# Cross attention with LoRA on one core: VectorE evicts each projected group one slot later in its order

## The reference

```python
def _lora_linear(x, W, A, B):
    return x @ W + SCALING * (x @ A @ B)
q = _lora_linear(hidden_states, Wq, Aq, Bq).reshape(bsz, q_len, NH, HD)
k = _lora_linear(traces, Wk, Ak, Bk).reshape(bsz, t_len, NKV, HD)
v = _lora_linear(traces, Wv, Av, Bv).reshape(bsz, t_len, NKV, HD)
...
scores = jnp.einsum('bhqd,bhtd->bhqt', q, k) / jnp.sqrt(jnp.asarray(HD, q.dtype))
attn = jax.nn.softmax(scores, axis=-1)
context = jnp.einsum('bhqt,bhtd->bhqd', attn, v)
out = _lora_linear(context, Wo, Ao, Bo)
return hidden_states + out
```

## Time and profile before

| | us |
|---|---|
| time, median of 3 runs (680.14 to 681.97) | 681.96 |
| time of the profiled execution | 681.03 |
| its span, first to last instruction | 678.9 |
| start-up and end outside the span | 2.1 |
| first T(4) to the last batch's T(4), seven batches | 414.3 |
| PE busy | 661.4 (97%) |
| DVE busy | 519.4 (77%) |
| ACT busy | 466.9 (69%) |

### The profile page before, as it was taken

How to read it: one execution, slowest core, us unless ns; L and a number is a source line. 1 busy time by engine, 2 the same in 40 slices (tenths; PEclk the granted TensorE clock), 3 DMA queues, 4 the chain that set the end, 5 groups by cost and what they waited for, 6 DMA issues and landing times.

```text
span 678.9 us, 14783 instructions
## 1 busy us (share of the span) xinstructions
PE 661.4 (97%) x4220; PEld 526.2 (78%) x4220; DVE 519.4 (77%) x1173; ACT 466.9 (69%) x1462; POOL 368.4 (54%) x316
## 2 busy tenths in 40 slices
PE   8999999999999999999999999999889999999998
PEld 6787777877887787787788788777666788888886
DVE  4868889788788778878877887878887898855542
ACT  5557888888888888888888888887678443222220
POOL 3548734852772484376258437635867005876632
PEclk9999999999999999999999999999999999999999
DMA  9957665774666477466657756667576234655331
GB/s 277 342 167 206 196 194 148 211 206 137 182 208 185 143 220 209 152 172 199 183 159 197 209 160 180 203 186 215 181 227 208 104 123 166 207 185 186 124 121 65
DMA packets 103797, 124.67 MB, mean 184 GB/s; under 512 B 9280, under 2 KB 85312, under 8 KB 103760
## 3 DMA queue, kind: packets, MB, share of 16 engines
q1 hardware_dynamic: 103760, 124.23, 60.5%
HBM read 86.18 MB, written 38.01 MB: 183 GB/s over the span
## 4 chain that ended last, share of the span: by engine, by line
PE 80%; DVE 9%; ACT 4%; DMA 3%; issue 2%; SPq 1%; POOL 0%; DVEq 0%; ACTq 0%; POOLq 0%
PE banks L1481 19%; PE banks L1674 17%; PE banks L1479 10%; PE banks L1499 8%; PE banks L1529 7%; PE banks L1516 7%; PE banks L1540 6%; DVE neg_max L1137 2%; ACT banks L906 2%; PE banks L1460 2%; PE banks L1446 2%; DVE turned_sb L1158 1%; PE banks L1447 1%; DMA q_parts<-q_stage 1%; DVE x_both L1178 1%
## 5 line engine op out<-in xcount | busy, mean ns | idle before, releaser
L906 ACT ACTIVATE banks<-banks,neg_max 128x256 f32<-128x256 f32 x512 | 230.2, 453 | 40.2 <-DVE neg_max L1137 32.4
L790 POOL TENSOR_TENSOR q_stack<-turned_sb,head_mask 8x512 fp32r<-8x512 f32 x128 | 138.5, 1082 | 185.3 <-DVE turned_sb L1158 179.1
L1137 DVE TENSOR_REDUCE neg_max<-banks 128x2 f32<-128x512 f32 x256 | 174.4, 684 | 30.1 <-PE banks L1499 28.7
L917 ACT ACTIVATE probs_t<-banks 128x512 f32<-128x512 f32 x256 | 155.1, 606 | 41.2 <-PE banks L1516 40.5
L1481 PE MATMUL banks<-x_both,w_hi 128*128 128x512 f32 x448 | 164.2, 398 | 1.1 <-DVE q_stage L1131 1.1
L1479 PE MATMUL banks<-x_both,w_lo 128*128 128x256 f32 x448 | 118.5, 280 | 0.0
L1499 PE MATMUL banks<-k_stack,q_stack 96*128 96x256 f32 x512 | 109.7, 296 | 2.1 <-DMA q_stack<-q_parts 2.0
L1499 PEld LDWEIGHTS banks<-k_stack,q_stack 96*128 96x128 f32 x512 | 80.7, 189 | 35.4 <-issue 17.6
L906 ACT ACTIVATION_READ_ACCUMULATOR banks<-banks,neg_max 128x1 f32 x512 | 107.3, 209 | 0.0
L1516 PE MATMUL banks<-q_stack,k_stack 104*128 104x512 f32 x256 | 101.6, 397 | 0.0
L1481 PEld LDWEIGHTS banks<-x_both,w_hi 128*128 128x128 f32 x448 | 83.1, 189 | 14.8 <-DVE q_stage L1131 3.4
(11 more groups left out here) (156 smaller groups left out, 1149.3 us busy)
## 6 DMA issues: line engine op xcount, KB each, us to landing
q_stack<-q_parts SPq DMA_DIRECT2D x192, 128.0 KB, 3.0
q_parts<-q_stage SPq DMA_DIRECT2D x64, 256.0 KB, 3.7
raw<-ct SPq DMA_DIRECT2D x32, 256.0 KB, 4.2
raw<-xt SPq DMA_DIRECT2D x32, 256.0 KB, 3.9
scales<-r_rows SPq DMA_DIRECT2D x64, 128.0 KB
context<-ctx_stage SPq DMA_DIRECT2D x64, 128.0 KB, 3.9
stage<-xn SPq DMA_DIRECT2D x16, 512.0 KB, 4.9
w_hi<-context SPq DMA_DIRECT2D x14, 512.0 KB, 7.0
```

The costliest lines, as they stand in the source:

```text
L790: nc.gpsimd.tensor_tensor(q_stack[rows, u % RING, heads], turned_sb[rows, u % 2].unsqueeze(1).broadcast_to([M_ROWS, 2, S]), head_mask[rows ...
L906: last = nc.scalar.activation(score_bank(s)[:, S * h:S * (h + 1)], score_bank(s)[:, S * h:S * (h + 1)], ACT.Exp, bias=neg_max[:, u % 2, i: ...
L917: nc.scalar.activation(probs_t[:, u % 2, t, 2 * hp:2 * hp + 2, :].rearrange("p a b -> p (a b)"), st_bank[j % 2], ACT.Exp, scale=-1.0).then ...
L1137: nc.vector.tensor_reduce(out=neg_max[:, u % 2, 2 * c:2 * c + 2], in_=score_bank(s).rearrange("p (h t) -> p h t", h=2), axis=AXIS, op=ALU. ...
```

## The change

In the first batch and in the loop, DVE evicts a group in slot e + 2 in place of e + 1, directly behind that slot's row maximum and ahead of everything else in the slot. The v1 group moves from the end of slot 3 to behind the row maximum of slot 4, in every batch, the last one too. The other groups of the last batch stay. No instruction is added or taken away, and PE, ACT, POOL and SP keep their order.

```diff
@@ proj_lows
-                    if end_slot(i, last) + 1 == s:
+                    if end_slot(i, last) + (1 if last else 2) == s:
@@ slot (vector)
                     row_max(b, s + AHEAD - 1)
-                if last:
-                    proj_lows(b, s, last)
+                proj_lows(b, s, last)
+                if s == FIRST + 1:
+                    (narrow_low if first else proj_low)("v", 1, 1, b * PER + (PRO - 1), None, b)
                 here = u >= 0 and not (last and u >= NG)
...
                 if s < FIRST:
                     return
-                if s == FIRST:
-                    (narrow_low if first else proj_low)("v", 1, 1, b * PER + (PRO - 1), None, b)
                 if first and s in LORA_O_SLOTS:
                     build_stack_o(LORA_O_SLOTS.index(s))
-                if not last:
-                    proj_lows(b, s, last)
-                    if s in LOW_SLOTS:
-                        j = LOW_SLOTS.index(s)
-                        input_low(x_hl, j, x_hi_done, x_ready, b * 4 + (j + 5))
+                if not last and s in LOW_SLOTS:
+                    j = LOW_SLOTS.index(s)
+                    input_low(x_hl, j, x_hi_done, x_ready, b * 4 + (j + 5))
```

## The result

The changed kernel takes 687.42 us (median of 4 runs, 686.77 to 688.73), the kernel before 681.69 us beside it (4 runs, 680.14 to 681.97). The ratio is 1.0096, 95% interval 1.0079 to 1.0112: slower by about 5.7 us, where 681.8 was forecast and 683.9 was the end of the range. The profiled execution of the changed kernel took 688.73 us, of which 2.2 lie outside its span, against 681.03 for the one of before: 7.7 us apart.

A forecast was written before the change was run, and what follows sets the result against it. PE, busy for 97% of the span at full clock, was taken as the bound. On the profiled 681.03 us, 3.5 - 1.5 - 1.0 - 0.3 + 0.1 = +0.8 us gave 681.8 us, range 679.6 to 683.9.

The forecast's parts named there:

- In the changed order slot 15 opens with its row maximum: Slots 15 to 19: DVE's gapless chain runs 0.18 us later, so k0's eviction makes slot 19's matmul 0.38 us late.
- The bound from above, 0.5: Slot 19: the most its matmul was expected to be late in a pass, in us, against 0.38 forecast.
- Slot 33 ... is the template of the changed slot.: Slot 33's v0 eviction already follows a row maximum; its timings, second start 0.61 us after the first, were applied to changed slots.
- step-0 price: Slots 11, 27 and 35: groups starting at step 0 begin 0.07 us late in each pass.
- The upper bound of 0.19: Slots 11, 27 and 35: the lateness in us if the matmul is delayed by as much as its load.
- Rival 3: Slower: the four step-0 starts pay the whole load's delay and slot 28's waits stay; 685.7 us at the far end; chance 0.20.
- Slot 24, -1.5 us: Loop, slot 24: the wait behind q0's eviction goes, since row maxima no longer queue behind it; 0.25 us in six passes.
- Slot 28, -1.0 us: Loop, slot 28: scores' waits for q0's stack shrink because slot 20's turning comes some 0.6 us earlier; bound: nothing goes.
- First batch, -0.3: First batch: slot 11 pays +0.6, slot 24's 0.48 goes, slots 27 and 32 keep half of 0.9; bounds -1.0 and +0.7.
- Last batch, +0.1: Last batch: the first fold waits 0.8 us longer for v1, less 0.66 us of the next fold's wait.
- Rival 5, Clock (0.02): Several small PE gaps a pass lower the granted clock to 1.2 GHz for one four-slot unit; at most 688 us; chance 0.02.
- What would show it: Right: alike passes of 58.9 to 59.2 us; wrong: differing passes, or slot 19's wait near zero or over 0.8 us.

The follow-up runs named there:

- turn_reversed: The changed kernel with DVE's four transposes of a unit in opposite order, the last one reading partitions 0 to 31; 685.01 us, ratio 1.0041.
- its control: The kernel before with only the order of its four turning instructions reversed; 681.32 us, ratio 0.9997.
- pool_after_low: The changed kernel, but GpSimd waits before its third input_high (slot 16) until DVE has done the first input_low; 687.42 us, ratio 1.0093.
- v1_early: The changed kernel, but v1 is evicted in slot 3 as before, in all batches; 690.13 us, ratio 1.0119.
- slack_late: The kernel before with only q4, q6, k1, q0, q2 and q3 evicted one slot late; 679.24 us, ratio 0.9984.
- v1_late_last: The kernel before, but in the last batch alone v1 is evicted in slot 4 behind the row maximum; 681.99 us, ratio 1.0015.

## Why the prediction was wrong, by its steps

- **"In the changed order slot 15 opens with its row maximum ..., does the same work, and is 0.18 later."** This is the step that failed. The chain from slot 15 to 19 was taken as a sum of DVE's own durations, moved as a block. It is not: moved by 0.30 us (T(15) + 2.12 for 1.82), its input_low asks for SBUF together with GpSimd's third high part (T(15) + 2.09) and lasts 1.56 us for 0.68 in four of the six passes. Slot 19 cost 5.8 us in the loop instead of 2.3. Of the 3.5 us missed the collision is 3.0 (four times 0.76), the hold of the next point the rest. Shown by the two kinds of pass, by the four passes of q7 late alone, and by turn_reversed, where input_low comes 0.18 late as predicted, the collision is gone and slot 19 costs 0.34. GpSimd's 3.60 us for three high parts stood in the trace of before; I never laid it beside DVE's timeline. The bound from above, 0.5, came from DVE and PE alone, so the range could not hold the truth.
- **"Slot 33 ... is the template of the changed slot."** Wrong for q: the eviction behind a row maximum starts 0.72 us after it, 0.61 for v. The step-0 price is 0.18 to 0.19 at slots 11 and 27 and 0.05 at slot 35, so 1.1 us each instead of 0.4. The same 0.11 us also carried input_low past GpSimd's start. The upper bound of 0.19 held. Shown by turn_reversed, with its control.
- **Rival 3, the nearest to what came**, set the same 0.19, but for another reason, the matmul delayed with its load. Its point of decision, a pass grown by 0.35 us, was passed (0.6 to 1.5 over the shortest pass). Its far end, 685.7, lay outside the range I gave; its "683.8 with half of it" is halfway from 681.8 to 685.7, not the sum with half of the 6.4, which is 682.5.
- **Slot 24, -1.5 us**: right in size, -1.7. That it follows from q0's own move is wrong: q0 late alone leaves 0.16 to 0.37, k0 late alone 0.04 to 0.11.
- **Slot 28, -1.0 us**: -0.4 in the trace of after, and 0.27 to 0.77 in some passes of the changed kernel with its turning reversed. I did not settle what sets it from pass to pass; the bound, that nothing goes, was right to be there, and was too kind. Of the eight traces with q0 late five lose 2.0 to 2.6 us there in the loop, the other three 0.5 to 1.2; the six with q0 in its old place lose 1.0 at most. The changed kernel's own trace, with 0.5, is at the lucky end.
- **First batch, -0.3**: -0.6, close by luck: slot 11 gave back 0.4 where +0.6 was in the sum, and slot 19 cost 0.6 that was not in it. The cast of 1.36 us did not come back: the changed order puts a row maximum in its place, and the casts take 0.29 and 0.78. In kernels that keep DVE's order up to slot 9 it is there each time (1.36 or 1.37 in seven), so it belongs to an order, and is not chance.
- **Last batch, +0.1**: +0.1 where it is done alone, but +2.0 in the trace of after (0.85 at the fold, 1.1 behind it). The lateness came as worked out; the second fold's wait did go. What was put at nothing is the clock behind the longer wait: half for 3.4 us, and 1.8 us of time, by the same batch in pool_after_low.
- **Rival 5, Clock (0.02)**: it came together with the collision. Against it stood that PE waits of over 1 us at full clock were in the rows; the wait of the first fold grew from 0.88 to 1.66 us, and with that the argument was gone. Its mechanism, several small gaps a pass, did nothing: the loop has such gaps and keeps the full clock. Its price of a whole unit, 7 us, was too high.
- **What would show it**: "over 0.8 at slot 19" was named as a sign of a wrong prediction, and it came; so did passes that differ from each other, though not by late transfers as said there.

## What to carry to other kernels

When a block of one engine's work is moved, lay the timeline of the engine it shares SBUF with beside it, and move one against the other. A start that shifts by 0.3 us can meet an instruction that it used to miss, and the price is nearly the whole of that instruction (0.88 us of 1.04), far above the shift. And where two such instructions start within 30 ns of each other, an edit elsewhere decides which pays: judge it by the durations in the trace, since the time of a kernel that undoes one part may say the opposite. Where PE's matmuls are slow and wait for nothing, read the granted clock in stretches of a few microseconds: a page of 40 slices shows a 9 over a slice with 3.4 us of half clock in it.

## What the runs showed of the hardware

- Two instructions, one of DVE with two SBUF inputs and one of GpSimd, started 20 to 30 ns apart and ran nearly one after the other; either may be the one to wait (DVE 1.56 for 0.68 us, GpSimd 1.60 for 1.04). It reaches down to a cast of eight columns (0.56 for 0.17 in pool_after_low; 0.16 or 0.17 in all 14 traces where no GpSimd instruction ran beside it). A row maximum from PSUM beside the same GpSimd work kept its 0.68.
- A DVE instruction behind a row maximum starts 0.61 us after the maximum's start, ahead of its end (0.69), or 0.72 after it, by which partitions its neighbours read; the order of four transposes decides 0.11 us.
- Behind a wait of PE of 1.66 us the granted clock fell to half for 3.4 us in three traces of the five with that wait, and a context product of 16 small matmuls took 1.70 to 1.94 us for 1.07. The same happened behind waits of 1.48 us (v1_early), 1.69 us (q7 late alone) and 2.17 us (slack_late). Waits of 1.66 and 1.67 us in pool_after_low and v1_late_last left it full, so such a wait does not always bring the fall.
